# One batch of an attention and feed-forward kernel in another order: the last batch takes the lower query half of all head groups first, and its tails follow each other every 11 steps

## The reference

```python
def reference(x, Wq, bq, Wk, bk, Wv, bv, Wo, bo, W1, b1, W2, b2):      # x: (16, 1024, 256) fp32
    q, k, v = heads(x @ Wq.T + bq), heads(x @ Wk.T + bk), heads(x @ Wv.T + bv)   # 16 heads of 16
    q, k = rope(q) * 16 ** -0.5, rope(k)
    a = softmax(q @ k.T) @ v                       # for each batch and head, 1024 queries and keys
    x = layernorm(x + merge(a) @ Wo.T + bo)
    h = relu(x @ ternary(W1).T + b1)               # 256 -> 1024
    return layernorm(x + h @ ternary(W2).T + b2)   # 1024 -> 256
```

## Time and profile before

| | |
|---|---|
| median of 3 runs | 3323.97 us (3323.8 to 3325.73) |
| profiled execution, first to last instruction | 3316.4 us |
| PE busy | 3242.7 us (98%) |
| DVE busy | 2990.2 us (90%) |
| ACT busy | 2530.5 us (76%) |
| POOL busy | 2147.2 us (65%) |
| mean granted TensorE clock | 0.990 |

### The profile page before, as it was taken

The page is one execution under the profiler, slowest core; times in us unless marked ns, Lnnn a source line. Parts: engine busy times, 40 slices in busy tenths (PEclk is TensorE's granted clock), DMA queues, the critical chain, the costliest instruction groups (busy, mean ns, idle before and its releaser), DMA issues. The chain is left out here.

```text
span 3316.4 us, 81549 instructions
## 1 busy us (share of the span) xinstructions
PE 3242.7 (98%) x30726; PEld 1773.5 (53%) x30726; DVE 2990.2 (90%) x5721; ACT 2530.5 (76%) x4971; POOL 2147.2 (65%) x2440
## 2 busy tenths in 40 slices
PE   7989999999999999999999999999999999999997
PEld 4434555555555555555555555555555555544445
DVE  7888999999999999999999999999999999999965
ACT  3777777777777777777777777777777777777773
POOL 2575766766766766766766766766766776754435
PEclk7999999999999999999999999999999999999989
DMA  8444454454355345355355345345345345344211
GB/s 220 100 96 103 96 116 103 96 116 107 93 115 109 91 115 111 89 115 111 94 114 118 88 109 118 92 105 119 94 106 116 96 104 116 98 95 80 55 38 57
DMA packets 312553, 341.20 MB, mean 103 GB/s; under 512 B 77280, under 2 KB 260448, under 8 KB 312160
## 3 DMA queue, kind: packets, MB, share of 16 engines
q1 hardware_dynamic: 311584, 335.20, 44.2%
q10 hardware_dynamic: 576, 0.79, 0.2%
HBM read 195.37 MB, written 140.51 MB: 101 GB/s over the span
## 5 line engine op out<-in xcount | busy, mean ns | idle before, releaser
L1071 DVE TENSOR_REDUCE mxp<-ms 128x1 f32<-128x512 f32 x4064 | 2614.6, 681 | 245.5 <-PE ms L749 200.7
L897 ACT ACTIVATE prob<-sc 128x512 f32<-128x512 f32 x4096 | 2225.1, 597 | 655.4 <-PE sc L760 629.6
L760 PE MATMUL sc<-qa,ka 50*128 50x512 f32 x4096 | 1545.2, 444 | 27.5 <-ACT prob L897 27.1
L749 PE MATMUL ms<-ka,qa 48*128 48x512 f32 x4064 | 1536.7, 446 | 2.9 <-DVE mxp L1289 2.2
L760 PEld LDWEIGHTS sc<-qa,ka 50*128 50x128 f32 x4096 | 684.5, 185 | 1115.8 <-ACT prob L897 962.6
L777 PE MATMUL ob<-prob,v_sb 128*17 128x512 f32 x8192 | 1081.9, 600 | 2.4 <-ACT at_st L904 2.3
L749 PEld LDWEIGHTS ms<-ka,qa 48*128 48x128 f32 x4064 | 679.4, 185 | 10.4 <-DVE mxp L1071 4.5
L1402 POOL TENSOR_TENSOR ve<-mv,eps_sb 128x2 f32<-128x2 f32 x119 | 23.2, 195 | 493.1 <-DVE mv L1098 493.1
L1423 POOL TENSOR_TENSOR hid_r<-hid,hid_r 128x512 fp32r<-128x512 f32 x240 | 308.6, 1286 | 19.2
L777 PEld LDWEIGHTS ob<-prob,v_sb 128*17 128x17 f32 x8192 | 136.0, 95 | 258.4 <-issue 258.1
L597 PEld LDWEIGHTS job<-h_t,w_sb 64*128 64x128 f32 x3840 | 261.3, 186 | 23.4
(11 more groups left out here) (157 smaller groups left out, 2833.6 us busy)
## 6 DMA issues: line engine op xcount, KB each, us to landing
qk_parts<-parts SPq DMA_DIRECT2D x122, 512.0 KB, 4.2
ka<-qk_parts SPq DMA_DIRECT2D x378, 128.0 KB, 4.6
qa<-qk_parts SPq DMA_DIRECT2D x378, 128.0 KB, 7.4
attention<-at_st SPq DMA_DIRECT2D x128, 256.0 KB, 3.3
v_ones<-v_st SPq DMA_DIRECT2D x64, 272.0 KB, 2.4
v_sb<-v_ones SPq DMA_DIRECT2D x64, 272.0 KB, 8.5
xn<-x SPq DMA_DIRECT2D x64, 256.0 KB, 4.8
ao<-attention SPq DMA_DIRECT2D x128, 128.0 KB
```

Source lines behind the costliest of these rows:

```text
L749: nc.tensor.matmul(ms[upto(b, g, NS1, at) % MS_BANKS][:, :], operand(qa, b, g, j, ROWS)[:, qt * P:(qt + 1) * P], operand(ka, b, g, j, ROWS ...
L760: nc.tensor.matmul(sc[upto(b, g, HG * STEPS, n) % SC_BANKS][:, :], operand(ka, b, g, j, ROWS + MROWS)[:, tt * P:(tt + 1) * P], operand(qa, ...
L897: nc.scalar.activation(prob[st_ % 2][:, j, :], sc[upto(b, g, HG * STEPS, n) % SC_BANKS][:, :], ACT.Exp).then_inc(s["exp_done"], 1)
L1071: nc.vector.reduce_max(mxp[(b * G + g) % 2][:, kh, j * TT + qt:j * TT + qt + 1], ms[upto(b, g, NS1, at) % MS_BANKS][:, :], AX.X).then_inc( ...
```

## The change

The last batch runs in another order. Its eight half units take the lower query half of head groups 0 to 3, then the upper half of head groups 0 to 3 (`half_at`); before, each group took both halves in turn. So the q and k rows of all four groups are needed at once, for which a fourth slot of `qa` and `ka` is made, and the values are loaded eight times and not four. Attention of tokens 0 to 511 is complete after step 32 of the 64. The tails in this batch begin every 11 steps (`LAST_PERIOD`), at steps 0, 11, 22, 33 for batch 14 and at steps 44 and 55 for the quarters 0 and 1 of batch 15; `t3a` and `t3b` now stand in one step. Tail (15, 1) ends behind the last step, and the dense form is used for tails (15, 2) and (15, 3) alone.

```diff
+LAST_PERIOD = 11
+LAST_JOBS = {0: ("t3a", "t3b"), 5: ("t4",), 7: ("f0",), 8: ("f1",), 9: ("f2",), 10: ("f3",),
+             12: ("g0",), 13: ("g1",), 14: ("g2",), 15: ("g3",)}
+LAST_FIRST_NORM = {(0, 2): "sum 0", (0, 3): "sum 1", (1, 2): "stats 0", (2, 2): "stats 1", (3, 0): "moments 0"}
+LAST_SECOND_NORM = {(15, 1): "sum 0", (15, 2): "sum 1", (16, 1): "stats 0", (16, 3): "stats 1", (18, 0): "moments 0"}
+def half_at(b, g, qh):
+    at = QH * g + qh
+    return (at % G, at // G) if b == B - 1 else (g, qh)
+def last_tail(k):
+    return B - 2 + k // G, k % G
+def last_tails_at(step):
+    return [(k, step - LAST_PERIOD * k) for k in range(G + 2) if step >= LAST_PERIOD * k]
...
-        qa = [sb(f"qa{i}", [P, HALF, S], fp32r) for i in range(RING)]
+        qa = [sb(f"qa{i}", [P, HALF, S], fp32r) for i in range(RING + 1)]
...
+                if (b, g) == (B - 2, G - 1):
+                    load_rows(B - 1, 2, slice(0, S), qk_loaded[slot_of(B - 1, 2)])
...
+            def last_batch():          # SP
+                load_rows(b, G - 1, slice(0, S), qk_loaded[slot_of(b, G - 1)])
...
+                store_attention(b, G - 1, 1)
+                tail_out(b, 0)
+                attention_in(b, 2)
+                tail_in(b, 3)
+                attention_in(b, 3)
+                for g in range(1, G):
+                    tail_out(b, g)
...
-                        if last and (g, st_) == (G - 1, STEPS - 2):
-                            pe.wait_ge(s["s1_taken"], B * G * NS1)
-                            whole(tail_job, b, 0, "t3 0", [], True)
...
-            frees = tail_job(end, 0, "t4", 0, [("t6_taken", upto(end, 0, TL, 0))], True)
+            frees = run(("tail", (end, 1), "f2"), frees)
             weigh(end, G - 1, STEPS - 1)
+            for name in ("f3", "g0", "g1", "g2", "g3"):
+                frees = run(("tail", (end, 1), name), frees)
...
+            frees = whole(tail_job, end, 2, "t3", frees, True)
+            frees = tail_job(end, 2, "t4", 0, frees, True)
-            for g in range(G):
+            for g in range(2, G):
...
+            last_batch()               # DVE
+            for p in range(2):
+                take_hidden(B - 1, 1, 2 + p, job[1][:, p * TQ:(p + 1) * TQ])
+            invert(B - 1, 2)
+            last_second_sums(1, job)
+            last_second_moments(B - 1, 1)
+            last_first_sums(2)
+            last_first_moments(2)
+            last_second_norm(B - 1, 1)
+            last_first_norm(2)
+            invert(B - 1, 3)
+            take_last_low(2)
...
+            last_batch()               # POOL
+            for n in (2, 3):
+                split_hidden(B - 1, 1, n)
+            normalise(B - 1, 2)
+            last_power(B - 1, 1, ve2, rstd2, "2_done")
+            last_power(B - 1, 2, ve, rstd, "_done")
+            normalise(B - 1, 3)
+            sum_x(B - 1, 3)
+            for g in range(2, G):
                 sum_h1(B - 1, g)
                 split_last_hidden(g, 0)
```

More of the change, by code:

```diff
@@ L139, in tile_of, with operands_of @@
     return HALF * upper + k // (TT // 2) % HALF, k // TT * (TT // 2) + k % (TT // 2), n % 2
+def operands_of(b, g, n):
+    j, qt, kh = tile_of(n)
+    unit, half = half_at(b, g, qt // (TT // QH))
+    return unit, j, half * (TT // QH) + qt % (TT // QH), kh
 def wait_used(engine, semaphore, count):
@@ L277, in build @@
         s = {n: sem(n) for n in names}
-        qk_loaded = [sem(f"qk_loaded{i}") for i in range(RING)]
+        qk_loaded = [sem(f"qk_loaded{i}") for i in range(RING + 1)]
         v_loaded = [sem(f"v_loaded{i}") for i in range(2)]
@@ L313, in banks_of @@
                 return ms[0], ob
-            if end and name == "t3 0":
-                return ms[0], ms[1]
             return job
@@ L474, in tail_out, with unit @@
                              ).then_inc(s["out_stored"], 16)
-            def unit(b, g, tail, last, first, tail_before):
+            def unit(b, g, tail, first, tail_before):
                 proj = projected(b, g)
@@ L817, in batch @@
                                 weigh_before(b, g, st_, first)
+                return free
             pe.wait_ge(s["ones_set"], 1)
@@ L1054, in _ @@
             take_outputs(B - 1, G - 1, 1)
-            take_last_norm(0)
-            for g in range(G):
+            finish(("tail", (B - 1, 1), "f3"))
+            finish_rest(("tail", (B - 1, 1), "f3"))
+            take_last_norm(2)
+            for g in range(2, G):
                 for n in range(FT // 2):
@@ L1526, in unit @@
                     split_hidden(b - 1, g, 3)
-                if not (last and g == G - 1) and len(proj) < 2:
+                if len(proj) < 2:
                     split_maxima(b + (g + 1) // G, (g + 1) % G, 0)
@@ L1546, in _ @@
             pool.wait_ge(s["powers_set"], 3)
-            for i in range(2 * RING):
+            for i in range(2 * RING + 2):
                 if i == 0:
```

209 lines of the change are left out of this document (129 added, 80 removed).

## The result

| | before | after |
|---|---|---|
| median | 3323.80 us (9 runs, 3316.37 to 3327.86) | 3334.15 us (9 runs, 3328.57 to 3339.88) |
| ratio after to before | | 1.0035, 95% interval 1.0025 to 1.0044 |
| span of the profiled execution | 3316.4 us | 3332.3 us |
| mean granted clock | 0.990 | 0.986 |

The change made the kernel 0.35% slower: 10.4 us between the medians, where 2.3 us faster was forecast. Slower by over 0.2% had a chance of 0.13, and the time is outside the range. In the runs shown with the result a run's time is its span plus 1.8 us, so the execution of before from which all rows of the prediction come took about 3318.2 us, 5.6 us less than its median. The spans therefore stand 15.9 us apart, the medians 10.4.

A forecast was written before the change was run, and what follows sets the result against it. Bound: a loop of exponential, score tiles and `weigh`, 3.08 us a step. Last batch 204.0 to 208.3 (+4.3), behind it 64.4 to 57.5 (-6.9): span 3313.8, plus 7.6 to the median, 3321.5 us; 8-in-10 range 3314.5 to 3330.

The forecast's parts named there:

- the extra loads: Unit (14, 3), SP's queue: twelve added loads push the first four transfers behind them by about 5 us, harmlessly.
- Jobs in 58 of 64 steps: Last batch: DVE and POOL work of six tails in place of four, +1.5 us (0 to 3).
- Pairs: Last batch: `t3a` and `t3b` in one step, six times at 1.2 us, +7.2 us (3.6 to 12).
- `g0` one step later: Last batch: `g0` needs DVE's second residual sum, now later, in four tails; +0.6 us (0 to 4).
- Clock in steps 60 to 62: End of last batch: some 8 us of low clock in emptier steps, +3 us (0 to 6).
- the old fall: Last unit of the kernel before: low clock from about 3211.2 to 3228.0, expected to go, -6.0 us.
- Behind the attention: Last exponential to the end: 57.5 us in place of 64.4, -6.9 us.
- The way through memory: Tail (15, 2), last copy to end of `att_t`: exposed stores and loads through multiplication, 11.3 us.
- rival 1: Behind the attention: a second clock fall while PE waits adds 3.6 us, giving 3325.1; chance 0.2.
- POOL's order: First layer of (15, 2) to that of (15, 3): POOL's queue delays the second split, +3.0 us, 16.9 in all.
- Rival 3: Steps 0 to 51 of last batch: DVE becomes the bound, 0.2 us a step, 10 us, 3332; chance 0.13.
- Rival 2: Last batch: pairs cost 3.6 instead of 7.2 us and clock stays up in steps 60 to 63, 3314.9; chance 0.25.

The follow-up runs named there:

- loads late: Changed kernel with the twelve added loads of unit (14, 3) issued behind the move of maxima, no longer ahead of it; 3325.74 us, 1.0009 of the kernel before.
- before with the loads alone: Kernel before plus the fourth slot, its two fills and the twelve loads ahead of the move of maxima, read by nothing; 3330.44 us, ratio 1.0026.
- the mended run: Changed kernel with loads behind the maxima, `weigh` later in steps 1 and 9 of a unit, and the reciprocal one step later; 3319.21 us, 0.9995 of before.
- pair apart: Changed kernel with `t3b` moved behind the fourth score tile of its step and DVE's two sums one and two places later; 3335.15 us, 1.0042 of before.
- before with idle pairs: Kernel before with three idle matmul pairs in each of three steps of its last unit, and `weigh` behind the fourth score tile there; 3318.02 us, ratio 0.9989.
- all waits filled: The mended run's kernel plus idle matmul pairs in PE's waits behind the attention, including two later waits of tail (15, 2); 3316.03 us, 0.9985 of before.
- the one other order tried: Changed kernel with POOL doing `h1b` of (15, 2) first, then `normalise` of (15, 3), two splits, its sum last; 3336.75 us, 1.0041 of before.
- The last three runs: Idle pairs in waits behind the attention on the mended run's kernel (0.9990), the same with more waits filled (0.9985), idle pairs in the kernel before (0.9989).

## Why the prediction was wrong

**The step that failed** is the one on the extra loads: "they push the first four by about 5 us, and none of these is due before a quarter of the unit later". It priced SP's issue time and four transfers, and stopped there. The fifth item behind the loads, the move of maxima, was not priced at all. Its issue was not late (15.0 us into the unit, as with the loads late); what came late was its landing. It had 24 loads of 128 KB ahead of it in place of 12, one lands every 1.0 us, and so it could be read back 12.3 us after its issue in place of 2.5. The Trainium skill says ("DMA: Bandwidth & Descriptors", Queues, rings and completion order) that each engine consumes descriptors in ring order; the landings in the trace agree, one load after the other from 3002.5 to 3025.8. The score tiles of step 8 need these rows at once, and PE stood 6.14 us. Loads late and before with the loads alone show it from both sides: 7.1 us gone, 5.9 us come. That is more than the whole distance from forecast to no change, and with the loads late alone the median of 3325.74 us lies inside the range.

**Where the rest is.** The span after is 18.5 us over the forecast 3313.8: 2.0 ahead of unit (14, 3), 7.8 in it, 5.3 in the last batch (213.6 for 208.3), 3.4 behind it (60.9 for 57.5). The median is off by less, 12.7 us. The prediction added 7.6 us between span and median, and 5.8 of these are only that the profiled execution of before was one of the quicker ones; that hid a part of the error in the spans. The items follow in the order of the prediction.

**Jobs in 58 of 64 steps: +1.5.** Split in two. The density itself is right as far as the remainder tells: the mended run has 206.1 - 196.0 - 6.9 - 1.7 = 1.5 us left for it. Missed were two orders in the queues that the mended run takes out, 4.7 us together (210.8 - 206.1). In steps 1 and 17, which now have no job, `weigh` follows the second score tile and meets ACT's copy: 2.6 us with the steps behind. The reciprocal at (5, 3) waits for `den`, which SP issues behind the move of maxima in step 5 and behind a store and a value load in step 49: 2.1 us.

**Pairs: +7.2.** Measured 6 x 1.15 = 6.9: right in size, for a partly wrong reason. Of the 1.15, pair apart puts 0.3 down to the drain that I named and 0.85 to the work.

**`g0` one step later: +0.6.** It was 0.42 in four steps, 1.7.

**Clock in steps 60 to 62: +3.** It did not fall there (steps 60 to 63: 3.08, 2.84, 3.18, 2.63 us). In this profile it fell in step 7 and around step 17 instead, 2.7 us (213.57 - 210.82, since loads late has the same waits without the falls). That this is close to the 3 us forecast is luck. What was taken off for the old fall, 6 us, was right, and before with idle pairs agrees that it came from the emptier steps.

**Behind the attention: 57.5.** Measured 60.9. The last copy ends 3274.72 - 3271.40 = 3.3 us behind the last exponential, as worked out. The way through memory, copy to end of `att_t`, took 11.8 in place of 11.3. By the Trainium skill's 2.0 us for each of four small transfers ("DMA: Bandwidth & Descriptors", the cost components, which the page fits to transfers issued by GpSimd; these are issued by SP) it would have been shorter still; the rows after have 2.2, 2.9, 1.4 and 3.7, and don't bear that out. From the end of `att_t` to the first layer the run with all waits filled takes 8.3 us and the changed kernel 9.5; from first layer to first layer they take 17.4 and 19.4. The difference, 3.2 us, is an estimate of what rival 1, the low clock in the wait, cost, and rival 1 said 3.6. At full clock the pieces are then 3.3 + 11.8 + 8.3 + 17.4 + 16.9 = 57.7, against 57.5 forecast. The +3.0 for POOL's order was right in size (17.4 against 16.9 forecast), and the second split ended 9.7 us behind the first layer where 9.9 was forecast. That POOL's order is the cause is not shown: the one other order tried brought nothing. The last stretch took 16.9, where 16.8 was forecast and 0.7 more for a fall that cost nothing there.

**The rivals.** Rival 3 named the other side and missed its mechanism: DVE did not become the bound, since steps without one of the places above take 3.09 us. Rival 2 came half true, the clock staying up in the last steps. With the loads, `weigh` and the reciprocal mended the same change is at 0.9995 of before, which is the forecast's "within 0.2%"; its span of 3316.0 stands against 3313.8 forecast. In that span the errors partly cancel: the last batch is 2.2 us shorter than forecast, what follows it 3.5 us longer.

**The clock, from both sides.** The Trainium skill ("TensorE: Matmul & The Clock Gate", What's actually happening) ties the clock to PE's recent work. The last three runs agree: filled waits kept it at 1.00. The busy time of the profile alone doesn't tell, though. In the last unit of the kernel before, PE was busy for 5.98 of the 7 us from 3204 to 3211 and the clock fell; it then stayed at 0.50 for 17.1 us, although PE was busy for 16.4 of them. (The 92% that the prediction gives for this fall is for a window that lies half behind it.) With idle tiles in one half of the array the fall came behind an open wait of 1.9 us. Whether the half or the wait mattered stays open, because the pairs filled both halves and the wait at once. Before with idle pairs shows that the fall in the last unit goes away when these steps are filled. There 2.6 of 6.0 us came back later, and in before with the loads alone a shorter fall in the last unit (2.1 us won) also went with more low clock behind it (2.9 us lost).

## What to carry to other kernels

When a change adds bulk loads, go down the issuing queue to every small transfer behind them and ask when its landing is due, not when its issue is: what is in the queues ahead of it counts in full. When a table of jobs is moved, look at the steps that become empty as well as at those that fill, since other work is placed by them. Where the clock falls in the waits near the end of a kernel, a few idle matmuls there can keep it up: pairs in both halves of the array did so here, single tiles in one half did not, and they must be few enough that the awaited operation finds PE free. The gain here was about 0.1%, in the new order (0.9995 to 0.9985 of the kernel before) as in the old one (0.9989).

## What the hardware showed beyond that

- From the first store of `maxima` (two of 16 KB) to the issue of the read behind them it took 2.5 us with the queues free and 12.3 us behind 24 loads of 128 KB, with the DMA share at 1.04 and 136 GB/s moved.
- Loads of 128 KB issued every 0.47 us landed one every 1.0 us in the order of issue, and a load of 256 KB behind 24 of them landed 16.2 us after its issue, 3.5 us behind 12.
- In the wait of 5 to 6 us that this made on PE the clock fell each time, in five executions, for 6.8 us, which the nine others don't have.
- With the same instructions in the third unit of the program, ten profiled executions had the clock low there once, which cost 2.4 us, and four did not. Single falls came also in the fourth unit (two executions) and in unit (14, 2) (three). What decides this wasn't tried.
